# A six-phase macaron kernel: in its two feed-forward phases, x enters PSUM by an identity matmul, one scale per block, and layer norm statistics joined on GpSimd three groups ahead

## The reference

```python
def fp4_quant_dequant(x):                       # blocks of 16 along the last dim
    scale = jnp.max(jnp.abs(xb), axis=-1, keepdims=True) / 6.0
    scale = jnp.maximum(scale, jnp.float32(1e-12))
    xn = xb / scale
    idx = jnp.searchsorted(_MID, jnp.abs(xn))   # nearest of 0, .5, 1, 1.5, 2, 3, 4, 6
    q = _GRID[idx] * jnp.sign(xn) * scale
...
gate = fp4_linear(x, w_gate)                    # 128 -> 352
y = fp4_linear(x, w_up)                         # 128 -> 352
h = jax.nn.silu(gate) * y
return fp4_linear(h, w_down)                    # 352 -> 128
...
x = x + 0.5 * _L1_ffn_ref(_layernorm(x, axis=-1), w_gate, w_up, w_down)   # twice: blocks 4 and 6
```

## Time and profile before

| | |
|---|---|
| Median of 3 runs | 862.58 us (860.27 to 863.15) |
| The profiled execution: own time, span of its trace | 863.56 us, 861.8 us |
| Busy in the span | PE 706.7, DVE 669.7, ACT 464.0, POOL 153.4 us |
| First and last product of silu and up (L1095) of `ffn_a` begin | 428.85 and 542.45 us |
| Last residual (L1069) of `ffn_a`, of `ffn_b` begin | 561.26 and 858.22 us |

### The profile page before, as it was taken

How to read it: one execution, slowest core, us unless ns; L and a number is a source line. 1 busy time by engine, 2 the same in 40 slices (tenths; PEclk the granted TensorE clock), 3 DMA queues, 4 the chain that set the end, 5 groups by cost and what they waited for, 6 DMA issues and landing times.

```text
span 861.8 us, 17411 instructions
## 1 busy us (share of the span) xinstructions
PE 706.7 (82%) x6034; PEld 533.9 (62%) x6034; DVE 669.7 (78%) x1674; ACT 464.0 (54%) x891; POOL 153.4 (18%) x319
## 2 busy tenths in 40 slices
PE   5999997898997999999567577659999855867774
PEld 3777765677776677777355466425786653546654
DVE  2887888366656678889799998749998856999995
ACT  3877786646461577777546445354333115644552
POOL 4010030554632010100111120021100011112100
PEclk9999999799998899999768878878999987677888
DMA  7000000000000000000000000000000000000000
GB/s 199 2 0 0 0 1 2 3 3 2 0 3 3 1 1 0 0 0 1 2 0 0 0 0 0 1 0 1 1 0 0 1 1 0 13 12 12 12 24 25
DMA packets 13453, 6.99 MB, mean 8 GB/s; under 512 B 1176, under 2 KB 13408, under 8 KB 13408
## 3 DMA queue, kind: packets, MB, share of 16 engines
q1 hardware_dynamic: 11328, 5.33, 2.3%
q10 hardware_dynamic: 2080, 1.05, 0.5%
HBM read 4.28 MB, written 2.10 MB: 7 GB/s over the span
## 4 chain that ended last, share of the span: by engine, by line
PE 64%; DVE 23%; issue 8%; ACT 3%; POOL 1%; DMA 0%; DVEq 0%; POOLq 0%; ACTq 0%
PE ps L1185 56%; PE ps L1503 4%; DVE ffn_work L722 3%; DVE ffn_work L727 2%; DVE picked L911 2%; PE ps L1516 2%; DVE hq L733 1%; DVE shared L1009 1%; DVE xn L733 1%; ACT xn L430 1%; DVE ffn_work L716 1%; DVE fq_x_max L699 1%; PE ps L1193 1%; DVE attT L917 1%; DVE picked L906 1%
## 5 line engine op out<-in xcount | busy, mean ns | idle before, releaser
L1185 PEld LDWEIGHTS ps<-w_sb,sq_h 128*128 128x128 f32 x1024 | 132.2, 193 | 70.3 <-ACT sq_h L452 51.5
L823 DVE SCALAR_TENSOR_TENSOR x_sb<-ps,gates,x_sb 128x128 f32 (+1 forms) x512 | 147.4, 344 | 20.1 <-PE ps L1185 12.5
L1185 PE MATMUL ps<-w_sb,sq_h 128*128 128x128 f32 x1024 | 138.4, 279 | 1.5 <-ACT sq_h L452 1.4
L1185 PE MATMUL ps<-xnT,w_sb 128*128 128x512 f32 x256 | 136.0, 615 | 0.0
L308 POOL TENSOR_SCALAR vareps<-meanvar 128x4 f32<-128x4 f32 (+1 forms) x44 | 25.0, 569 | 619.8 <-DVEq L767 619.4
L448 ACT ACTIVATE relu_h<-ps 128x512 f32<-128x512 f32 x128 | 75.7, 591 | 60.1 <-PE ps L1185 59.8
L430 ACT ACTIVATE xn<-x_sb,shift,rstd 128x128 f32 (+1 forms) x192 | 79.8, 481 | 23.4 <-POOL shift L316 23.4
L452 ACT ACTIVATE sq_h<-relu_h 128x512 f32<-128x512 f32 x128 | 80.6, 630 | 4.0
L1516 PE MATMUL ps<-ident,xn 128*128 128x128 f32 x64 | 16.8, 414 | 70.8 <-DVE xn L733 70.8
L1185 PE MATMUL ps<-downT,hqT 128*128 128x128 f32 x384 | 71.0, 339 | 0.5 <-ACT hqT L630 0.5
L1185 PEld LDWEIGHTS ps<-downT,hqT 128*128 128x128 f32 x384 | 63.5, 245 | 7.4 <-ACT hqT L630 5.8
(11 more groups left out here) (148 smaller groups left out, 1265.8 us busy)
## 6 DMA issues: line engine op xcount, KB each, us to landing
x_sb<-in_L_attn_x_dram SPq DMA_DIRECT2D x8, 256.0 KB, 6.9
out_dram<-x_sb SPq DMA_DIRECT2D x8, 256.0 KB, 2.3
w_sb<-in_L_ffn_w_all_dram ACTq DMA_DIRECT2D x2, 512.0 KB, 5.9
wraw<-in_L_attn_qkv_w_dram SPq DMA_DIRECT2D x1, 192.0 KB, 4.9
wraw<-attn_in_proj_weight_dram SPq DMA_DIRECT2D x1, 192.0 KB, 4.1
fraw<-in_L_ffn_w_down_dram SPq DMA_DIRECT2D x1, 176.0 KB, 3.1
fraw<-in_L_ffn_w_gate_dram SPq DMA_DIRECT2D x1, 128.0 KB, 2.9
fraw<-in_L_ffn_w_up_dram SPq DMA_DIRECT2D x1, 128.0 KB, 2.6
```

The lines of the kernel that those rows point to most:

```text
L823: t = nc.vector.scalar_tensor_tensor(tile_b(i, j), bank(4 + e % 4, TPB, C)[:, j, :], gates[:, j, e:e + 1], tile_b(i, j), ALU.mult, ALU.add)
L1185: return nc.tensor.matmul(o, a, b, start=start, stop=stop, **kw)
```

## The change

Five things change, all inside `ffn` and the weights that it uses:

- x by the identity. `x_under(i)` on PE writes x of the group (512 columns) into bank 7 by an identity matmul before the down products, which then accumulate on it (`start=False`). `residual` on DVE goes; `x_out(i)` on ACT copies bank 7 to `x_sb`, after the last `hidden_T`.
- One scale a block. `scales` (two operations) becomes `nudged_scales` (one), whose result serves the way back and, through the reciprocal, the division. Sign, the half and the small enlargement go into the weights, as the `scale` of the three copies of `fp4_weights_out`.
- Layer norm. For groups 2 to 7 `bn_aggr` goes; DVE only takes the halves (`halves`), and POOL joins them in `ln_from_halves`, ten operations in place of four.
- Ahead. The halves are taken for group i+3 behind the x4 division, before `snap` of h4 (group 2: between the two `x_alone`); ACT does `normal(i+3)` between the second and third `hidden_T`, and `normal(2)` before the first `silu_up`.
- PE turns x behind the first two hidden transposes, no longer ahead of them.

```diff
+            def ln_from_halves(s, i, n):
+
+                half = stats[:, 0:n, :]
+                mean_sum, mean_gap, gap_sq, spread, var = [sums[:, k, 0:n] for k in range(5)]
+                base = 6 + 9 * (i - 2)
+
+                def step(k, ins):
+                    ins.then_inc(s["pool_chain"], 1)
+                    return k + 1
+
+                pool.wait_ge(s["var_ready"], i + 1)
+                pool.sem_inc(s_passed_pool, 1)
+                k = step(0, nc.gpsimd.tensor_tensor(mean_gap, half[:, :, 1], half[:, :, 4], ALU.subtract))
+                k = step(k, nc.gpsimd.tensor_tensor(mean_sum, half[:, :, 1], half[:, :, 4], ALU.add))
+                k = step(k, nc.gpsimd.tensor_tensor(spread, half[:, :, 2], half[:, :, 5], ALU.add))
+                pool.wait_ge(s["pool_chain"], base + 1)
+                pool.sem_inc(s_passed_pool, 1)
+                k = step(k, nc.gpsimd.tensor_scalar(gap_sq, mean_gap, 0.5, None, ALU.mult))
+                pool.wait_ge(s["pool_chain"], base + 3)
+                pool.sem_inc(s_passed_pool, 1)
+                k = step(k, nc.gpsimd.tensor_scalar(var, spread, 1.0 / C, LN_EPS, ALU.mult, ALU.add))
+                pool.wait_ge(s["pool_chain"], base + 4)
+                k = step(k, nc.gpsimd.tensor_tensor(gap_sq, gap_sq, gap_sq, ALU.mult))
+                k = step(k, nc.gpsimd.tensor_scalar(negmean[:, 0:n], mean_sum, -0.5, None, ALU.mult))
+                pool.wait_ge(s["pool_chain"], base + 6)
+                k = step(k, nc.gpsimd.tensor_tensor(vareps[:, 0:n], var, gap_sq, ALU.add))
+                pool.wait_ge(s["pool_chain"], base + 8)
+                k = step(k, nc.gpsimd.tensor_tensor(rstd[:, 0:n], vareps[:, 0:n], minus_half[:, 0:n], ALU.pow))
+                pool.wait_ge(s["pool_chain"], base + 9)
+                nc.gpsimd.tensor_tensor(shift[:, 0:n], negmean[:, 0:n], rstd[:, 0:n],
+                                        ALU.mult).then_inc(s["rstd_ready"], 1)
...
+                elif ph in ("ffn_a", "ffn_b"):
+                    ln_group(s, 0, TPB)
+                    ln_group(s, 1, TPB)
+                    with pool.Fori(2, GROUPS) as i:
+                        ln_from_halves(s, i, TPB)
...
-                nc.scalar.activation(gateT[:, :], bank(3, FK), ACT.Copy).then_inc(s_prep_act, 1)
+                nc.scalar.activation(gateT[:, :], bank(3, FK), ACT.Copy, scale=-(1.0 - NUDGE)).then_inc(s_prep_act, 1)
...
-                nc.scalar.activation(downT[:, :, :], bank(5, 3, P), ACT.Copy).then_inc(s_prep_act, 1)
+                nc.scalar.activation(downT[:, :, :], bank(5, 3, P), ACT.Copy, scale=-0.5 * (1.0 - NUDGE)).then_inc(s_prep_act, 1)
...
                     act.wait_ge(s["htr_done"], i * TPB + j + 1)
                     nc.scalar.activation(hqT[:, j % 2, :, :], bank(5 + j % 2, 3, P), ACT.Copy).then_inc(s["hT_ready"], 1)
-                def body(i, ahead, last):
-                    if ahead:
-
-                        act.wait_ge(s["tr_done"], i + 2)
-                        normal(i + 2)
+                def x_out(i):
+                    act.wait_ge(s["down_done"], i * TPB + TPB)
+                    act.sem_inc(s_passed_act, 1)
+                    nc.scalar.activation(group_b(i), bank(7, TPB, C), ACT.Copy).then_inc(s["x_done"], 1)
+
+                def body(i, ahead, last, further):
                     act.wait_ge(s["h_divided"], i + 1)
                     magnitude(fq_h[0], fq_h[1]).then_inc(s["h_sized"], 1)
                     if not last:
                     if not last:
                         silu_up(i + 1, 2)
                         silu_up(i + 1, 3)
+                    hidden_T(i, 0)
+                    hidden_T(i, 1)
                     if ahead:
                         evac_xnT(s, i + 2)
-                    for j in range(TPB):
-                        hidden_T(i, j)
+                    if further:
+                        normal(i + 3)
+                    hidden_T(i, 2)
+                    hidden_T(i, 3)
+                    x_out(i)
                 if not first:
                     normal(0)
                 x_magnitude(0)
                 evac_xnT(s, 0)
                 x_magnitude(1)
+                normal(2)
                 for j in range(TPB):
                     silu_up(0, j)
                 evac_xnT(s, 1)
-                with act.Fori(0, GROUPS - 2) as i:
-                    body(i, True, False)
-                body(GROUPS - 2, False, False)
-                body(GROUPS - 1, False, True)
+                with act.Fori(0, GROUPS - 3) as i:
+                    body(i, True, False, True)
+                body(GROUPS - 3, True, False, False)
+                body(GROUPS - 2, False, False, False)
+                body(GROUPS - 1, False, True, False)
...
-                def inverse(self):
+                def nudged_scales(self):
                     self.ch.need(self.t)
-                    self.t = self.ch.add(nc.vector.reciprocal(self.rs, self.rs))
+
+                    self.t = self.ch.add(nc.vector.tensor_scalar(self.sl, self.mx, (1.0 + NUDGE) / 6.0, 1e-12,
+                                                                 ALU.mult, ALU.max))
+
+                def inverse(self, of=None):
+                    self.ch.need(self.t)
+                    self.t = self.ch.add(nc.vector.reciprocal(self.rs, self.rs if of is None else of))
...
-                def residual(i):
-
-                    dve.wait_ge(s["down_done"], i * TPB + TPB)
-                    nc.vector.scalar_tensor_tensor(group_b(i), bank(7, TPB, C), 0.5, group_b(i),
-                                                   ALU.mult, ALU.add).then_inc(s["x_done"], 1)
-
                 def x_stream(i):
                     start = TPB if type(i) is int and i == 1 else 0
                     xflat = xn[:, start:start + TPB, :].rearrange("p j f -> p (j f)")
...
                     dve.wait_ge(s["xn_ready"], i + 1)
                     x4 = x_stream(i)
                     x4.largest()
-                    x4.scales()
-                    x4.inverse()
+                    x4.nudged_scales()
+                    x4.inverse(x4.sl)
                     x4.divide()
                     x4.snap()
                     x4.unbias()
                     x4.rescale()
-                def body(i, ahead, behind):
-
-                    if ahead:
-                        ln_stats(s, ch, i + 2, TPB, tile_b)
+                def halves(i):
+
+                    for j in range(TPB):
+                        t = nc.vector.bn_stats(stats[:, j, :], tile_b(i, j))
+                    t.then_inc(s["var_ready"], 1)
+
+                def body(i, ahead, further):
                     dve.wait_ge(s["up_ready"], i * TPB + TPB)
                     nc.vector.tensor_tensor(hflat, silu_g[:, :, :].rearrange("p j f -> p (j f)"),
...
                              s["h_divided"], s["h_sized"], i + 1, s["hq_ready"])
                     dve.wait_ge(s["hid_done"], i + 1)
                     h4.largest()
-                    h4.scales()
-                    h4.inverse()
+                    h4.nudged_scales()
+                    h4.inverse(h4.sl)
                     h4.divide()
-                    if behind:
-                        residual(i - 1)
                     if ahead:
                         dve.wait_ge(s["xn_ready"], i + 3)
                         x4 = x_stream(i + 2)
                         x4.largest()
-                        x4.scales()
-                        x4.inverse()
+                        x4.nudged_scales()
+                        x4.inverse(x4.sl)
                         x4.divide()
+                    if further:
+                        halves(i + 3)
                     h4.snap()
                     h4.unbias()
                     if ahead:
...
                     dve.wait_ge(s["xn_ready"], 1)
                     ln_stats(s, ch, 1, TPB, tile_b)
                 x_alone(0)
+                dve.wait_ge(s["xn_ready"], 2)
+                halves(2)
                 x_alone(1)
                 pre = ch.k
-                ch.start(pre)
-                body(0, True, False)
-                pre += ch.k
-                with dve.Fori(1, GROUPS - 2) as i:
-                    ch.start((i - 1) * PER["ffn"] + pre)
+                with dve.Fori(0, GROUPS - 3) as i:
+                    ch.start(i * PER["ffn"] + pre)
                     body(i, True, True)
                     assert ch.k == PER["ffn"], ("ffn", ch.k)
-                pre += (GROUPS - 3) * PER["ffn"]
-                ch.start(pre)
-                body(GROUPS - 2, False, True)
-                body(GROUPS - 1, False, True)
+                ch.start((GROUPS - 3) * PER["ffn"] + pre)
+                body(GROUPS - 3, True, False)
+                body(GROUPS - 2, False, False)
+                body(GROUPS - 1, False, False)
...
+                def x_under(i):
+
+                    if not (type(i) is int and i == 0):
+                        pe.wait_ge(s["x_done"], i)
```

(13 more changed lines are left out.)

## The result

| | before | changed |
|---|---|---|
| Median of the runs | 862.87 us (860.27 to 863.18, 4 runs) | 851.87 us (851.14 to 852.39, 4 runs) |
| Ratio, 95% interval | | 0.9879 (0.9858 to 0.9899) |
| Span of the profiled execution, mean granted clock | 861.8 us, 0.895 | 849.9 us, 0.938 |

What follows compares the result with a forecast made beforehand. The prediction took DVE to set the feed-forward loop's pace. Its terms, -11.3 + 2.7 + 3.5 = -5.1 us a phase, -10.2 for both, took the profiled 863.56 to 853.4; forecast 853 us (850 to 857), chance 0.42.

Steps and rivals of the forecast that it cites:

- term of -11.3 a phase: Feed-forward loop and tail: DVE spared residual, part of statistics and one scale, 1.9 us per body with statistics.
- One operation of POOL to a boundary of DVE: Loop: one POOL operation gets in between successive two-input DVE instructions at no DVE cost; seven of ten are held.
- The term +2.7: Loop: POOL's late rstd delays ACT's magnitude; DVE waits 0.6 us in alternate bodies, 1.4 in body 5; +2.7 a phase.
- Ahead of the loop: Before body 0: `normal(2)` makes the first silu 4.5 us later, the body's start 2.5 to 4.9; 3.5 taken.
- The tail: After the last product: the residual becomes a copy on ACT and one scale goes, -0.3 us a phase.
- 1: Loop: POOL's chain isn't late, rstd comes before the turned x; -15.6 us, about 847; chance 0.18.
- 3: Loop: the run of seven DVE instructions holds POOL as a whole; +7 us a phase, 877; chance 0.12.
- 4: Prologue costs 4.9 us or more and ACT's waits come in each body; within 2 us, about 862; chance 0.08.
- 2: Hidden part stays at 1.2 GHz, or DVE pays 0.1 per boundary with POOL; +4 us a phase, about 861; chance 0.20.

Runs made afterwards that it cites:

- the kernel with both edits: Changed kernel with `normal(i+3)` behind the fourth `hidden_T` and `normal(2)` behind the first gate, up and x copies: 843.44 us, ratio 0.9766 to the kernel before.

## Why the prediction was right, step by step

**DVE.** "A body with statistics would last 15.2" is the measured 15.22, body 6 "12.2" is 12.22, and DVE was the limit wherever nothing waited. This term of -11.3 a phase, which held -0.3 for the tail, is confirmed but for the tail.

**POOL.** One operation of POOL to a boundary of DVE, taken from the distant, was the right reading. With T the end of `rescale` (476.79 in body 2), the last held operation was to end at T + 3.0 and ended at 479.71, T + 2.9. rstd with shift was to be known at T + 4.6 (the terms given for it add to 4.7); rstd ended at 480.84 and shift at 481.11, T + 4.3, since the short operation that I had put behind the held ones got in between two of them. The magnitude was to end at T + 10.2 = 486.99 and ended at 487.01. The alternation of the waits came as foretold, with 0.38 in place of 0.6 (by the prediction's own times, T + 10.2 against T + 9.7, it would be 0.5), and body 5 waited 1.16 to the foretold 1.4. The term +2.7 came to 2.2: bodies 1 and 3 are 0.48 longer than 15.22, and body 5 is 15.67, where the kernel with both edits has 14.40 for it. The loop was to be 113.6 - 10.95 + 2.7 = 105.3 and was 104.96. The experiments on the length show that the chain was on the path, lightly, near a point where it becomes steep: +1.6 a loop for three more operations, +5.0 for six (a part of it by the clock), -1.5 and -1.7 for the short chain.

The rule of the Trainium skill, "SBUF — State Buffer", section "Who interferes with whom", was weighed there, and its two parts part ways here. That the second to come is held agrees with all seven held operations of the chain. That the first keeps the ports for its whole instruction is not seen for rstd. In body 2 above it can't be: rstd took 1.04 beside the maximum of h4 (L747), which reads one tensor. In the kernel with `normal(2)` later it took

```profile
453.95 2.35 POOL L350 TENSOR_TENSOR rstd<-vareps,minus_half 128x4 f32<-128x4 f32 x1
...
456.38 0.75 POOL L352 TENSOR_TENSOR shift<-negmean,rstd 128x4 f32<-128x4 f32 x1
```

held first by `snap` (453.78 to 455.41), and running on to 456.30, beside `unbias`, which started at 455.44 and took its usual 1.63:

```profile
455.44 1.63 DVE L781 SCALAR_TENSOR_TENSOR ffn_work<-ffn_work 128x1408 f32<-128x1408 f32 x1
```

**Ahead of the loop.** The step was right in kind: the first silu is 3.8 us later in both phases. 4.5 was foretold, because `normal(2)` was to start 10.4 us behind the first x4 maximum and started at 9.8. ACT and PE caught up 1.9 us of it in `ffn_a`, at a granted clock of 1.00, and 0.2 in `ffn_b`, at 0.68. The result, +1.9 and +3.6, has a mean of 2.7, where 3.5 was taken from a range of 2.5 to 4.9; the first lies below it. That the clock held in `ffn_a` was luck, as far as the prediction goes: in three kernels with the same prologue it didn't, and the term was +3.6 there too, near the 3.5 foretold.

**The tail** had the wrong sign: +0.33 in `ffn_b` and +0.38 in `ffn_a` (last product to the first BN_STATS behind the last group's x, 20.03 for 19.65), for -0.3. The copy on ACT replaced the residual as expected, but the transposes and down products of the last group took 6.81 us at a granted clock of 0.65 (549.20 to 556.01), and before 6.31 at 0.71 (554.91 to 561.22).

**The rest.** By these steps a phase gained 5.6 us, on the mean of the two, for the 5.1 foretold: 6.34 in `ffn_a` (1.92 - 8.64 + 0.38 = -6.34) and 4.86 in `ffn_b`. That makes -11.2; the untouched phases came out at -0.7 together: +1.1 ahead of `ffn_a`, and -1.8 in the attention, where a stretch of its start was granted a higher clock. Before, and after:

```profile
570.00:587.00 17.00, 13.69 (x55) 6.41 (x57) 10.13 (x14) 9.86 (x18) 2.36 (x4) 0.70 0.00 0
```

```profile
564.80:581.00 16.20, 11.62 (x63) 5.69 (x65) 10.55 (x14) 9.89 (x18) 2.37 (x4) 0.91 0.01 2
```

In the spans the sum had -10.2 and -11.9 was measured. By the numbers above DVE's part was 0.1 off for both phases together; POOL's took 0.9 less than foretold, the prologues 1.5 less, the untouched phases gave 0.7, and the tail took 1.3 more. The 0.7 and the 1.7 of the clock in one prologue are no merit of the change or of the prediction; without them the median would be some 854.

The rivals: 1 fell, since ACT waits for POOL and DVE for ACT. 3 fell in this kernel. 4 fell, for each of its two mishaps. 2 fell in this kernel, though not because the clock was near 1.00 throughout, as the prediction expected: in bodies 3 and 5 of each phase it was 0.89, and the slow stretch was hidden behind ACT's `normal`. Its mechanism, a fall of the clock where PE waits some 2.5 us among the down products, is what the kernels with two scales and with `normal(2)` later showed, at 1.2 to 1.7 us in a body. Two tenths on DVE decided whether it came.

Most of my misses in the experiments have one cause. I added parts, where each changes what is late next. The residual was thought worth 5 to 7 us and was worth 12 to 15 (two loops of 6.76); the join 4, and was worth about nothing; the place of `normal` 4, and was worth 1.3 in the loops alone, nothing in the total, but 3.5 in the loops together with the other edit (847.27 to 843.44). In two others it is the clock: two scales again was thought worth 2 to 3 and was worth 5 to 8, x turned first 8 to 14 and was worth 4 to 7.

**What stays open**: why the clock falls behind one wait of 2.5 or 3.0 us and not behind another of the same length. The runs show both cases, in one body and another, in one phase and another of the same execution, and in one kernel and another for the prologue of `ffn_a`, but not what tells them apart.

## What to carry to other kernels

On an engine that sets the pace, count what each body is spared and then follow the next chain to its end with times: the body, its alternating waits and the end of the magnitude came out within 0.5 us that way here. Small operations that are moved to POOL beside two-input instructions of DVE took about as long as one DVE instruction each (0.64 to 1.58 us for 0.20), so put first the operations that the result needs, and keep the chain short. Ask where moved work stands in the prologue, since there the loop's cover is missing: moving `normal(2)` behind the first copies, with a shorter POOL chain, gave 9 to 13 us more, as much as the change itself. And before an edit is credited with a stretch, compare the granted clock there: 1.7 us of a prologue went with it here in kernels that didn't touch it.

## What the runs showed of the hardware that I had not expected

- The granted clock of TensorE is not a function of the instructions alone: two phases of one execution with the same work ran a body at 0.81 and at 1.00, behind waits of 2.99 and 2.98 us. The body was 1.5 us longer at the lower one. Nor does a lower clock always cost time: body 3 of the changed kernel, at 0.89, lasted 15.70 like body 1 at 1.00.
- A MEMSET of POOL (3.51 us, begun at 110.60 in the kernel before) did hold a DVE instruction: it stretched one TENSOR_SCALAR to 1.78 us, until 0.14 after the MEMSET's end, where it is 0.29 at 15.07. The median of the 16 such TENSOR_SCALAR is 0.28. Two-input instructions beside the MEMSET, four of them in 0.62 at 110.98, were as long as at 304.18, where POOL was idle.

```profile
110.60 3.51 POOL L360 MEMSET shared<- 128x4096 f32 x1
```

```profile
112.47 1.78 DVE L799 TENSOR_SCALAR diff<-diff 128x256 f32<-128x256 f32 x1
```
